# Small inversion steps of a gated delta rule: one product made per 32-row quarter instead of per 64-row half

## The reference, cut to what matters

```python
A = jnp.where(tri, 0.0, -jnp.einsum('bhncd,bhned->bhnce', kb, k))
for i in range(1, chunk):
    upd = jnp.einsum('...k,...kj->...j', A[..., i, :], A[..., :, :i])
    A = A.at[..., i, :i].add(upd)
inv = A + jnp.eye(chunk, dtype=A.dtype)
u = inv @ v
w = inv @ kb
```

## Time and profile before

| what | value |
|---|---|
| three runs | 5786.07, 5783.81 and 5801.77 us, median 5786.07 |
| span of the profiled execution | 5785.5 us, which is also its own time (the median lies 0.6 us above it) |
| instructions in the span | 94866, of them 39740 matmuls and 39740 weight loads on PE |
| PE busy | 4147.9 us, 72% |
| DVE busy | 2997.7 us, 52% |
| ACT busy | 1935.9 us, 33% |
| mean granted clock of PE | 0.754 of full speed |

### The profile page before, as it was taken

The page is one execution under the profiler, slowest core; times in us unless marked ns, Lnnn a source line. Parts: engine busy times, 40 slices in busy tenths (PEclk is TensorE's granted clock), DMA queues, the critical chain, the costliest instruction groups (busy, mean ns, idle before and its releaser), DMA issues.

```text
span 5785.5 us, 94866 instructions
## 1 busy us (share of the span) xinstructions
PE 4147.9 (72%) x39740; PEld 3210.4 (55%) x39740; DVE 2997.7 (52%) x7965; ACT 1935.9 (33%) x4236; POOL 817.3 (14%) x600
## 2 busy tenths in 40 slices
PE   6786969367787878873747767586777777776298
PEld 5675849255565555552636556474445555445277
DVE  4445352525545454557355555546666666665232
ACT  2233231223333333330232332424444554552122
POOL 0000000231110011101600000002111111110434
PEclk7555555588888898885756665667889898898599
DMA  9200000140000000001210000000000000000255
GB/s 261 51 1 1 2 1 2 55 158 1 1 1 1 1 1 1 1 1 36 29 41 2 1 1 2 0 2 2 1 1 1 1 1 1 1 1 17 70 158 142
DMA packets 140860, 152.33 MB, mean 26 GB/s; under 512 B 7808, under 2 KB 128002, under 8 KB 139792
## 3 DMA queue, kind: packets, MB, share of 16 engines
q1 hardware_dynamic: 119024, 128.21, 7.6%
q0 software_dynamic: 21408, 18.05, 1.8%
HBM read 87.38 MB, written 59.76 MB: 25 GB/s over the span
## 4 chain that ended last, share of the span: by engine, by line
PE 50%; DVE 29%; ACT 12%; issue 3%; POOL 2%; DMA 2%; another core or an unknown queue 1%; SPq 0%; DVEq 0%; POOLq 0%; ACTq 0%
PE banks_lane L801 4%; ACT work L3231 4%; PE banks_lane L422 3%; PE banks_lane L3668 2%; PE banks_lane L1885 2%; PE banks_lane L1251 2%; PE banks_lane L809 2%; PE banks_lane L3117 2%; PE banks_lane L3152 1%; PE banks_lane L950 1%; PE banks_lane L3139 1%; ACT work L1979 1%; PE banks_lane L3097 1%; DVE work L2793 1%
## 5 line engine op out<-in xcount | busy, mean ns | idle before, releaser
L422 PE MATMUL banks_lane<-constants,work 128*128 128x128 f32 x968 | 203.3, 360 | 495.8 <-DVE work L408 209.6
L422 PEld LDWEIGHTS banks_lane<-constants,work 128*128 128x128 f32 x968 | 154.6, 186 | 566.1 <-DVE work L408 197.5
L402 POOL TENSOR_TENSOR weights<-weights,constants 128x4 f32<-128x4 f32 x76 | 78.5, 1033 | 2032.1 <-DVE weights L397 2032.1
L422 PE MATMUL banks_lane<-constants,weights 128*128 128x128 f32 x596 | 125.8, 348 | 332.7 <-DVE weights L408 93.3
L3231 ACT ACTIVATE work<-banks_lane,weights 128x192 f32<-128x192 f32 (+1 forms) x512 | 249.0, 505 | 136.2 <-DVE weights L3328 136.1
L422 PEld LDWEIGHTS banks_lane<-constants,weights 128*128 128x128 f32 x596 | 89.2, 179 | 362.6 <-issue 166.5
L402 POOL TENSOR_TENSOR work<-work,constants 128x4 f32<-128x4 f32 x76 | 77.3, 1018 | 1200.0 <-DVE work L397 1200.0
L3335 POOL TENSOR_TENSOR weights<-weights,constants 128x16 f32<-128x16 f32 x64 | 185.4, 2896 | 377.8 <-DVE weights L3243 377.8
L3324 DVE TENSOR_REDUCE weights<-banks_lane 128x2 f32<-128x384 f32 (+1 forms) x256 | 122.5, 520 | 145.6 <-PE banks_lane L3139 145.6
L3152 PE MATMUL banks_lane<-constants,work 128*128 128x128 f32 x896 | 137.0, 299 | 80.2 <-DVE work L3316 42.7
L2032 DVE TENSOR_REDUCE work<-banks_lane 128x2 f32<-128x512 f32 x256 | 158.9, 685 | 68.1 <-PE banks_lane L1899 67.4
(11 more groups left out here) (779 smaller groups left out, 11121.1 us busy)
## 6 DMA issues: line engine op xcount, KB each, us to landing
work<-experts_dram_l_ffn SPq DMA_DIRECT2D x39, 964.0 KB
room_l_ffn<-work SPq DMA_DIRECT2D x30, 1188.0 KB, 15.0
work<-experts_dram_l_ffn SPq DMA_DIRECT2D x23, 512.0 KB
weights<-weights_dram SPq DMA_DIRECT2D x1, 4833.5 KB, 14.1
work<-room_l_ffn SPq DMA_DIRECT2D x36, 132.0 KB
weights<-weights_dram SPq DMA_DIRECT2D x1, 4112.0 KB, 12.8
weights<-bands_dram SPq DMA_DIRECT2D x1, 4096.0 KB, 13.2
weights<-room_l_ffn SPq DMA_DIRECT2D x26, 132.0 KB
```

Source lines behind the costliest of these rows:

```text
L402: pool.tensor_tensor(n.rstd, n.rstd, c("neghalf", cols=(0, n.rstd.shape[1])), ALU.pow).then_inc(*u.pool.step(name))
L422: done = pe.transpose(bank[0:rows, t * P:(t + 1) * P], block, c("ident"))
```

## The change

`strict` becomes half as wide and holds the four blocks of a matrix one below the other, 32 columns wide. The left product takes one 32-row quarter at a time. Level 0 reads `strict` directly, without the addition. The memset of `strict` goes.

```diff
-        self.strict = arena.take(INVERTED, 2 * SMALL)
-        self.strict_half = [self.strict[:, :, n * SMALL:(n + 1) * SMALL] for n in range(2)]
+        self.strict = arena.take(INVERTED, SMALL)
...
         dve.memset(self.XT, 0.0).then_inc(*u.dve.step())
-        dve.memset(self.strict, 0.0).then_inc(*u.dve.step("strict_cleared"))
...
             for m in range(INVERTED):
-                for g in map(half_of, range(2)):
-                    made = pe.matmul(b[2][g, m * SMALL:(m + 1) * SMALL], self.strict[g, m, :], self.x[g, m, :])
+                for q in map(quarter, range(QUARTERS)):
+                    made = pe.matmul(b[2][q, m * SMALL:(m + 1) * SMALL], self.strict[q, m, :], self.x[q, m, :])
             made.then_inc(*u.pe.step(f"left{pair}_{n}"))
...
         for i in range(QUARTERS):
-            act.copy(self.strict_half[i % 2][quarter(i)], self.NT8[quarter(i), :, quarter(i)]).then_inc(*u.act.step(f"strict{pair}"))
+            act.copy(self.strict[quarter(i)], self.NT8[quarter(i), :, quarter(i)]).then_inc(*u.act.step(f"strict{pair}"))
...
         dve.wait_ge(*u.act.at(f"strict{pair}"))
-        dve.tensor_tensor(self.part, *self.strict_half, ALU.add).then_inc(*u.dve.step())
-        dve.wait_ge(*u.dve.last())
-        dve.tensor_tensor(self.part, self.part, per_tile(self.c("small0"), INVERTED), ALU.mult).then_inc(*u.dve.step())
+        dve.tensor_tensor(self.part, self.strict, per_tile(self.c("small0"), INVERTED), ALU.mult).then_inc(*u.dve.step())
```

## The result

The changed kernel takes 5816.1 us (median of 9 runs, 5807.4 to 5823.6), and the kernel before, beside it on the same chip, 5786.1 us (9 runs, 5779.4 to 5801.8). The ratio is 1.0045, with an interval of 1.0034 to 1.0056: 0.45% slower, 26 us above the forecast of 5790 and inside the range. The difference of 30 us is more than the 17 us within which the forecast called two times the same. So "slower" came, to which it had given 0.36, and not "the same", to which it had given 0.52.

What follows compares the result with a forecast made beforehand. PE's instruction supply, 3.55 us per 256, was taken to bound dense stretches. Terms +30 (no fillers), -9 (addition), -17 (quiet fillers), +1 (first filler stretch), -1 (memsets) gave +4: 5790 us from 5785.5, range 5768 to 5826.

Steps and rivals of the forecast that it cites:

- Which limit: PE's instructions come in blocks of 256, one block ahead, at least 3.55 us per block; 345 transfers after the change.
- The rival by which instructions come in time: Block edges cause no loss, rounds without fillers take 3.64 us, 115 us less in all: 5671 us; chance 0.10.
- The new left product: On PE, 64 records on four quarters take 1.08 us, 0.85 from start to start, 0.84 us less each.
- the serial rival: The four quarters do not run side by side with 32 columns, 3.4 us per left product: about 5990 us; chance 0.02.
- Twelve stretches without fillers: Stretches without filler products: 21.4 against 19.5 us, +2.0 each, with +0.5 behind them; twelve times 2.5 is +30 us.
- the joining levels: After each stretch without fillers they start with the instruction buffer empty: +0.5 us, a guess between 0 and 1.
- the 5.5 periods of 3.55 us: In a stretch without fillers, 6 or 7 block edges are crossed, the first without a stop: 19.5 us.
- the 1.9 us for the instructions ahead of the first edge and behind the last: In a stretch without fillers, about 270 instructions outside the block periods, at 1.8 us per 256.
- The first edge without a stop: In a stretch without fillers PE has rested before, so the next block is there at the first edge crossed.
- The rival of the long period: 3.9 us per block instead of 3.55, 23 us in 66 periods and 8 in the first stretch: 5821 us; chance 0.18.
- L885: DVE addition removed ahead of left products: 0.46 us saved in four stretches without fillers, 0.85 in layer 2's eight, -9 us.
- Filler stretches: Stretches with filler products: three in quiet time -5.7 us each, -17 us; the first +1 us, between -7 and +9.

Runs made afterwards that it cites:

- the second experiment: Kernel before, with left products by quarters only in the three filler stretches after the first and by halves everywhere else: 5760.0 us, ratio 0.9970.

## Why the prediction was nearly right, and where it was not

**Which limit.** Right. PE's instructions come in blocks of 256, 345 transfers as counted, and the work taken from PE came back as "issue". The rival by which instructions come in time (5671 us) falls: rounds are 7.21 us, not 3.7. With it falls, for dense stretches of small matmuls, the rule in "Runtime: NRT & Kernel Launch" of the Trainium skill, "Instruction fetch mechanics", that crossing an edge is mostly hidden; the stops of 1.5 to 1.8 us in the chain above disagree with it.

**The new left product.** Right. 64 records in 1.08 us and 0.88 from start to start, forecast 1.08 and 0.85 (kernel after, timeline, PE, no fillers, then with fillers; it answers to the earlier trace rows):

```profile
3539.13 1.08 PE L799 MATMUL banks_lane<-work 32*32 32x32 f32 x64 [1.84 <-issue]
3540.01 1.06 PE L799 MATMUL banks_lane<-weights 32*32 32x32 f32 x64
```

```profile
612.50 1.08 PE L799 MATMUL banks_lane<-weights,work 32*32 32x32 f32 x64
613.50 1.46 PE L1247 MATMUL banks_lane<-weights 128*64 128x16 f32 x12
```

A filler product starts 1.00 us after the left product, against 1.85 before. The four quarters run side by side although they write one bank, so the serial rival (5990 us) falls too.

**Twelve stretches without fillers.** Right in sign, too small in size, and this is the step that put the centre too low. Measured as the forecast did, to the first record of the last right product, the stretches take 19.47 us on average before and 23.01 after: +3.5 us where +2.0 stood. The last right product and the joining levels behind it take 0.8 us more, where the guess was 0.5. That is +4.4 us against +2.5, in twelve stretches 22 of the 26 us.

Two terms of the sum were too small. The first is the 5.5 periods of 3.55 us, 19.5 us. The period was read from a single pair of transfers, to one slice of 0.275 us; from stop to stop it is 3.69 us. On average 5.7 whole blocks lie between the first and the last edge of such a stretch (3.65 us each, with those in which PE starts with work in stock), 20.7 us together. The second is the 1.9 us for the instructions ahead of the first edge and behind the last; this part takes 2.3 us. Here the forecast also counted wrong: 1,717 less 5.5 times 256 is 309 instructions, not 270, which is 0.3 us.

The first edge without a stop was right in the main. In eight of the twelve stretches the first stop comes only after 280 to 492 instructions, as in the one that begins at 437.97 (kernel after, PE; the first row comes after 454 instructions); in the other four there is a first stop of only 0.28 to 0.45 us, as at 3534.93 above.

```profile
443.36 0.56 PE L807 MATMUL banks_lane<-weights,work 32*32 32x16 f32 x27 [1.83 <-issue]
447.09 0.59 PE L799 MATMUL banks_lane<-weights,work 32*32 32x32 f32 x27 [1.51 <-issue]
```

The rival of the long period came out nearest in its time (5821 us). It had the direction right and the size wrong: 3.9 us per block is not what the transfers show, and 3.69 instead of 3.55 in its 66 periods is 9 us, not 23. One reading was off without effect on the sum: a left product before takes 1.78 us from start to start (3519.13 to 3522.69 in the earlier trace rows) and not 1.66; the sum goes by 1.86 us saved per pair, which is right.

**L885.** The places are right: the addition ahead of the mask is gone (the mask is now L883, the subtraction L885), and so the first lane's chain makes way for L2874 one step earlier (kernel after, DVE; it answers to the earlier trace rows):

```profile
3526.03 0.42 DVE L883 TENSOR_TENSOR weights<-weights,constants 128x256 f32<-128x256 f32 x1
3526.49 0.42 DVE L885 TENSOR_TENSOR weights<-constants,weights 128x256 f32<-128x256 f32 x1
3526.95 0.45 DVE L887 STREAM_TRANSPOSE weights<-weights 128x256 f32<-128x256 f32 x1
3527.43 0.42 DVE L2874 TENSOR_TENSOR work<-banks_lane,work 128x256 f32<-128x256 f32 x1
```

From the first lane's first left product to the second lane's it is 5.55 us on average before and 5.15 after, and in most stretches of layer 2 PE's wait ahead of the first lane's is shorter by 0.46 us (1.41 to 0.95, or 0.47 to 0.01). That they are worth 9 us in the total is not confirmed.

**Filler stretches.** Three in quiet time: -6.2 us each, forecast -5.7, and the second experiment, which has these three alone, is 16 us faster. The first: 47.6 us, measured to the last record, to 49.96 us, +2.4, forecast +1 (-7 to +9); the second experiment shows 51.6 us with the old left products, so the difference says little. There DMA moves 255 GB/s and the transfers are 5.0 us apart on average.

**The sum in the traces.** Windows of twelve stretches +50, their joining levels +2 (13.31 to 13.48 us each), quiet filler stretches -19, the first one +2.4, the shorter waits at L885 about -9, the memsets -1: about +26 us. The spans differ by 32.1 us. Of the rest, 2.5 us lie between the last stretch of layer 0 and the first of layer 2, and 2.3 us behind the last stretch, where nothing but the memsets was changed.

## What to carry to other kernels

On PE, count instructions as well as busy time: where small matmuls stand close together, 256 of them cost 3.7 us on average (3.45 to 4.03) however short each one is, so splitting a product into more and shorter ones pays only where longer instructions stand between them. To forecast such a stretch, take the period from many transfers, not from one pair, count to the last instruction that comes at that pace, and allow for what PE has in stock at the start. Here all instructions at 3.69 us per 256, less 2.1 us, give 24.7 us for the stretches of the changed kernel (24.60 measured) and 18.3 for those with half of the left products (18.46); the 2.1 us are fitted to these two. With half of the right products left out as well it would give 11.7, and 12.54 was measured: there DVE and the work itself count too. When only some places of a loop can gain from an edit, make it there alone: that turned 0.45% slower into 0.3% faster.

## What the runs showed of the hardware

- One block of 256 instructions ahead, no more: in the twelve stretches of the changed kernel the next transfer begins 1.0 to 1.7 us after PE has gone on, and the block is usable 2.2 to 3.0 us after its transfer began. Beside 255 GB/s of other transfers the distance grows from 3.7 to 5.0 us.
- 64 records with 32 by 32 stationary elements take 1.05 us with 16 moving columns and 1.08 with 32, on four quarters that write one bank, at a granted clock of 0.50; the moving columns hardly count between these two.
- Two lanes shifted against each other by 12 phases: 1.2% slower with long left products, 0.35% faster with short ones. I had expected it to help with both. The granted clock in layer 2 is 0.58 with the shift and long products, 0.61 with the shift and short ones, 0.62 without the shift.
